# Three rounded products for the attention's output projection, and a subtraction in the vector engine's queue

## What is computed

```
y = num / (den + 1e-6)                       # 16 heads x 64
y = (y - mean(y)) / sqrt(var(y) + 1e-9) * ln_w        # per head
x1 = x + ga * (y.reshape(16 * 64) @ w_proj)  # 1024 -> 256
h  = layernorm(x1) * (1 + cb) + sb
logits = h @ Wr.T                            # 8 experts
```

## Time and profile before

| | us |
|---|---|
| median of 3 runs | 2130.3 (2128.81 to 2131.07) |
| profiled execution, its own time | 2129.61 |
| its span in the profile | 2127.8 |
| PE, DVE, ACT, POOL busy over the span | 1949.6, 1793.2, 1286.0, 830.6 |
| `close_attention`, from the first folding matmul to the last logits copy | 1309.56 to 1525.00 |
| the loop's turns, from tile 8's L1381 to tile 31's | 1358.60 to 1495.45 |

### The profile page before, as it was taken

How to read it: one execution, slowest core, us unless ns; L and a number is a source line. 1 busy time by engine, 2 the same in 40 slices (tenths; PEclk the granted TensorE clock), 3 DMA queues, 4 the chain that set the end, 5 groups by cost and what they waited for, 6 DMA issues and landing times. The chain is left out here.

```text
span 2127.8 us, 37910 instructions
## 1 busy us (share of the span) xinstructions
PE 1949.6 (92%) x13199; PEld 1382.8 (65%) x13199; DVE 1793.2 (84%) x2652; ACT 1286.0 (60%) x2168; POOL 830.6 (39%) x729
## 2 busy tenths in 40 slices
PE   7999779999999999999999995999537999999993
PEld 6767535555555555555555553898526999999993
DVE  5999849999999999999999997777587777787783
ACT  4454357777777787777778772444204565566561
POOL 3777511121111112111111211566345666666563
PEclk9999879999999999999999997999757999999997
DMA  5887892355543345554334502444512443334444
GB/s 181 282 277 268 271 246 55 91 129 124 129 103 99 86 105 130 124 124 91 103 85 120 124 21 86 122 132 131 163 50 55 88 92 79 71 83 90 88 88 109
DMA packets 156104, 260.57 MB, mean 122 GB/s; under 512 B 44568, under 2 KB 120160, under 8 KB 149472
## 3 DMA queue, kind: packets, MB, share of 16 engines
q1 hardware_dynamic: 127792, 214.07, 36.0%
q0 software_dynamic: 15840, 22.29, 6.8%
q10 hardware_dynamic: 12304, 22.02, 3.1%
HBM read 162.40 MB, written 100.14 MB: 123 GB/s over the span
## 5 line engine op out<-in xcount | busy, mean ns | idle before, releaser
L998 ACT ACTIVATE att_sb_a<-att_ps_s,att_sb_fg,att_sb_f 128x1024 f32<-128x1024 f32 x384 | 454.4, 1202 | 230.4 <-PE att_ps_s L1143 219.4
L1036 DVE TENSOR_TENSOR keep_sb_store<-keep_sb_store,att_sb_a 128x1024 f32<-128x1024 f32 (+2 forms) x528 | 535.2, 1028 | 16.6 <-ACT att_sb_a L998 8.3
L954 POOL TENSOR_SCALAR_AFFINE_SELECT att_sb_dec<-att_sb_dec 128x128 f32<-128x128 f32 x256 | 178.7, 699 | 844.9 <-ACT att_sb_dec L988 844.9
L1162 PE MATMUL att_ps_off<-att_sb_a,att_sb_v 128*64 128x512 f32 x1520 | 365.5, 594 | 1.1 <-DVE att_sb_part L1063 1.1
L1795 ACT ACTIVATE ffn_sb_h<-ffn_ps_p,ffn_sb_b_cols 128x256 f32<-128x256 f32 x320 | 152.1, 477 | 168.1 <-PE ffn_ps_p L1986 167.4
L1900 DVE TENSOR_TENSOR ffn_sb_h_lo<-ffn_sb_h,ffn_sb_h_hi 128x256 fp32r<-128x256 f32 x320 | 213.2, 708 | 27.2 <-ACT ffn_sb_h_hi L1788 25.8
L1143 PE MATMUL att_ps_s<-att_sb_q,att_sb_k 64*128 64x512 f32 (+1 forms) x1896 | 229.9, 376 | 5.0 <-DMA att_sb_k<-k_rows 4.9
L1143 PEld LDWEIGHTS att_ps_s<-att_sb_q,att_sb_k 64*128 64x128 f32 x1896 | 159.1, 186 | 115.3 <-issue 63.6
L1143 PEld LDWEIGHTS att_ps_s<-keep_sb_late,att_sb_k 64*128 64x128 f32 x1920 | 160.4, 185 | 110.1 <-issue 56.6
L1143 PE MATMUL att_ps_s<-keep_sb_late,att_sb_k 64*128 64x512 f32 (+3 forms) x1920 | 230.8, 374 | 0.3
L1052 DVE SCALAR_TENSOR_TENSOR att_sb_a<-att_ps_s,att_sb_dec 128x1024 f32<-128x1024 f32 (+3 forms) x256 | 209.0, 817 | 7.7 <-PE att_ps_s L1143 5.3
(11 more groups left out here) (256 smaller groups left out, 3589.3 us busy)
## 6 DMA issues: line engine op xcount, KB each, us to landing
q_rows<-early_sb_halves SPq DMA_DIRECT2D x32, 1024.0 KB, 4.8
att_sb_k<-k_rows SPq DMA_DIRECT2D x60, 512.0 KB, 15.6
ffn_sb_raw<-L_ffn_W ACTq DMA_DIRECT2D x36, 512.0 KB
close_sb_nT<-num_rows SPq DMA_DIRECT2D x34, 512.0 KB, 4.0
k_rows<-early_sb_halves SPq DMA_DIRECT2D x16, 1024.0 KB, 4.9
keep_sb_late<-q_rows SPq DMA_DIRECT2D x32, 512.0 KB, 13.8
num_rows<-att_sb_num SPq DMA_DIRECT2D x64, 256.0 KB, 2.7
att_sb_hb<-half_log SPq DMA_DIRECT2D x15, 1024.0 KB, 22.9
```

What stands on the lines that cost most here:

```text
L954: nc.gpsimd.affine_select(out=tile, in_=tile, compare_op=ALU.is_ge, fill=0.0, base=0, pattern=[[1, P]], channel_multiplier=-1).then_inc(de ...
L998: nc.scalar.activation(x, s_ps[slot(op)][:, :, :], ACT.Square, scale=f[:, p, i - 1, s:s + 1], bias=fg[:, p, i - 1, s:s + 1]).then_inc(sq_d ...
L1036: nc.vector.tensor_tensor(x[:, :, c:TB], x[:, :, c:TB], y[:, :, c:TB], ALU.max).then_inc(max_done, 1)
L1162: last = nc.tensor.matmul(ps[h * HD:(h + 1) * HD, c:TB], v_tile, a[:, a_slot(op), h, c:TB], start=(s == 0), stop=(s == (ST * i if kind == ...
```

## The change

The output projection is computed from three rounded products. `yT` is split into `yT_hi` (ACT's copy, now rounding to float32r) and `yT_lo` (a new subtraction on DVE, `py` minus `yT_hi`, 128x1024). The weights are split into `w_hi` and `w_lo` likewise, by one more DVE instruction for each of the four folded parts. PE does 24 matmuls on float32r in place of eight on float32, of the same shape. PE's next transposes into `py` now wait for the subtraction, as does the projection. In DVE's queue the subtraction stands ahead of the sum of squares. The copy of the logits, which stood there, moves to the end of ACT's turn.

```diff
@@ ACT's turn
-                    nc.scalar.activation(yT[:, p, :, :], py[:, :, :], ACT.Copy).then_inc(yT_done, 1)
+                    nc.scalar.activation(yT_hi[:, p, :, :], py[:, :, :], ACT.Copy).then_inc(yT_hi_done, 1)
...
+                if there[7]:
+                    act.wait_ge(l_mm, ready(n - 7))
+                    apart(act, keep)
+                    nc.scalar.activation(keep.logits[:, n - 7, :], pl[:, :], ACT.Copy).then_inc(l_done, 1)
...
+            act.wait_ge(l_done, ready(NTT - 1))
@@ DVE's fold
-                    nc.vector.tensor_copy(w[:, 2 * g:2 * g + 2, :], pw[:, :, :]).then_inc(folded, 1)
+                    nc.vector.tensor_copy(w_hi[:, at, :], pw[:, :, :]).then_inc(rounded, 1)
+                    dve.wait_ge(rounded, g + 1)
+                    nc.vector.tensor_tensor(w_lo[:, at, :], pw[:, :, :], w_hi[:, at, :].bitcast(F32), ALU.subtract).then_inc(folded, 1)
@@ DVE's turn
-                if there[7]:
-                    dve.wait_ge(l_mm, ready(n - 7))
-                    apart(dve, keep)
-                    nc.vector.tensor_copy(keep.logits[:, n - 7, :], pl[:, :]).then_inc(l_done, 1)
+                if there[2]:
+                    dve.wait_ge(yT_hi_done, ready(n - 2))
+                    dve.wait_ge(a_mm, free(n - 2, 2))
+                    nc.vector.tensor_tensor(yT_lo[:, p, :, :], py[:, :, :], yT_hi[:, p, :, :].bitcast(F32),
+                                            ALU.subtract).then_inc(yT_lo_done, 1)
                 if there[0]:
                     dve.wait_ge(sq_done, ready(n))
@@ PE's turn
-                    pe.wait_ge(yT_done, free(n - 2, 1))
+                    pe.wait_ge(yT_lo_done, free(n - 2, 1))
...
-                    pe.wait_ge(yT_done, ready(n - 3))
+                    pe.wait_ge(yT_lo_done, ready(n - 3))
                     pe.wait_ge(gx_done, free(n - 3, 1))
-                    for j in range(KVH):
-                        last = nc.tensor.matmul(pa[:, :], yT[:, 1 - p, j, :], w[:, j, :], start=(j == 0), stop=(j == KVH - 1))
+                    terms = [(a, b, j) for a, b in ((yT_hi, w_hi), (yT_hi, w_lo), (yT_lo, w_hi)) for j in range(KVH)]
+                    for o, (a, b, j) in enumerate(terms):
+                        last = nc.tensor.matmul(pa[:, :], a[:, 1 - p, j, :], b[:, j, :], start=(o == 0), stop=(o == len(terms) - 1))
```

More of the change, by code:

```diff
@@ L1181, in close_attention @@
         w_raw = m.sbuf("w_raw", [P, KVH, D])
-        w = m.sbuf("w", [P, KVH, D])
+        w_hi = m.sbuf("w_hi", [P, KVH, D], F32R)
+        w_lo = m.sbuf("w_lo", [P, KVH, D], F32R)
         basis_sb = m.sbuf("basis", [P, P])
@@ L1193, in close_attention @@
         y = m.sbuf("y", [P, 2, HEADS, HD])
-        yT = m.sbuf("yT", [P, 2, KVH, P])
+        yT_hi = m.sbuf("yT_hi", [P, 2, KVH, P], F32R)
+        yT_lo = m.sbuf("yT_lo", [P, 2, KVH, P], F32R)
         gx = m.sbuf("gx", [P, 2, D])
@@ L1209, in close_attention @@
         pw = m.psum("pw", [P, 2, D])
-        w_in, scaled, fold_mm, folded, wr_mm, wr_done, eps_done = (
-            m.sem(s) for s in ("w_in", "scaled", "fold_mm", "folded", "wr_mm", "wr", "eps"))
+        w_in, scaled, fold_mm, rounded, folded, wr_mm, wr_done, eps_done = (
+            m.sem(s) for s in ("w_in", "scaled", "fold_mm", "rounded", "folded", "wr_mm", "wr", "eps"))
         n_in = [m.sem(f"n_in{i}") for i in range(2)]
@@ L1214, in close_attention @@
         h_out = [m.sem(f"h_out{i}") for i in range(2)]
-        n_mm, num_done, sq_done, var_done, std_done, r_done, y_done, y_mm, yT_done, a_mm = (
-            m.sem(s) for s in ("n_mm", "num", "sq", "var", "std", "r", "y", "y_mm", "yT", "a_mm"))
+        n_mm, num_done, sq_done, var_done, std_done, r_done, y_done, y_mm, yT_hi_done, yT_lo_done, a_mm = (
+            m.sem(s) for s in ("n_mm", "num", "sq", "var", "std", "r", "y", "y_mm", "yT_hi", "yT_lo", "a_mm"))
         gx_done, x1_done, var2_done, std2_done, xn_done, hs_done, h2_done, h_mm, hT_done, l_mm, l_done, head_chain, norm_chain, mod_chain = (
@@ L1274, in _ @@
         def _(act):
-            for s in (sq_done, std_done, yT_done, std2_done, hT_done):
+            for s in (sq_done, std_done, yT_hi_done, std2_done, hT_done, l_done):
                 act.sem_inc(s, CREDIT)
@@ L1333, in _ @@
         def _(dve):
-            for s in (num_done, var_done, r_done, gx_done, var2_done, xn_done, l_done):
+            for s in (num_done, var_done, r_done, gx_done, var2_done, xn_done, yT_lo_done):
                 dve.sem_inc(s, CREDIT)
@@ L1357, in fold @@
                 for g in parts:
+                    at = slice(2 * g, 2 * g + 2)
                     dve.wait_ge(fold_mm, g + 1)
-                    nc.vector.tensor_copy(w[:, 2 * g:2 * g + 2, :], pw[:, :, :]).then_inc(folded, 1)
+                    nc.vector.tensor_copy(w_hi[:, at, :], pw[:, :, :]).then_inc(rounded, 1)
+                    dve.wait_ge(rounded, g + 1)
+                    nc.vector.tensor_tensor(w_lo[:, at, :], pw[:, :, :], w_hi[:, at, :].bitcast(F32), ALU.subtract).then_inc(folded, 1)
                 if g == KVH // 2 - 1:
```

## The result

The changed kernel takes 2141.43 us (median of 5 runs, 2141.01 to 2143.55), the kernel before 2130.3 us (median of 5, 2128.81 to 2132.72) beside it: a ratio of 1.0054, 95% interval 1.0039 to 1.0068. The change makes the kernel slower by 11.1 us. The profiled execution took 2142.37 us by its own time, with a span of 2140.6 us, 12.8 us more than before.

What follows compares the result with a forecast made beforehand. PE was taken to set the loop's pace at 5.95 us a turn, DVE nearly equal. Loop +18.4, before it +4.4, behind it -0.5 gave +22.3 us, a forecast of 2152.6 us, range 2142 to 2164.

Steps and rivals of the forecast that it cites:

- DVE sets the pace: In the loop: DVE's turn becomes 6.75 us and bounds it; PE's saving of 0.55 us goes into idle time.
- The growth of DVE's turn, 0.80: In the loop: each DVE turn grows from 5.95 to 6.75 us, 0.76 for the subtraction plus 0.04.
- the loop's term: Over the loop's 23 turns, 0.80 us each: +18.4 us.
- The 0.76: In DVE's turn: the sum begins at 1409.92 instead of 1409.16, the subtraction starting where the logits copy did.
- The 0.04 allowed for one more wait: In DVE's turn: a guessed 0.04 us for the one more wait that its queue must evaluate.
- I take these gaps as DVE's own: nothing PE does would close them: DVE's loop idle time, gaps between dependent steps and 0.36 us marked issue, is not slack behind PE.
- DVE's gaps close: Rival, in the loop: issue gaps are covered, the turn grows by 0.4 us, 2143 us in all; chance 0.12.
- The cover of the high part: In the loop: yT_hi is ready 0.5 us before the subtraction wants to begin, so that wait costs nothing.
- the ring that the prediction walked through once, as a check: In the loop: sum, ACT's L1297, logits copy, hT, PE's logits matmuls and transposes of y; yT_hi ready at 2.0 to 2.1.
- Before the loop, +4.4: Ahead of the loop: folded weights +2.3, turns 2 to 4 +0.1, turns 5 and 6 +1.6, turn 7 +0.4 us.
- Behind the loop, -0.5: After the loop: later start and moved copy cost 1.1 us, three shorter projections save 1.65.
- The clock: PE's granted clock stays at 1.00 in the loop; rival: it falls, 2175 to 2245 us, chance 0.05.

Runs made afterwards that it cites:

- e3_dve_alone: Changed kernel with the projection back in eight plain float32 matmuls, the subtraction kept on DVE but its result unused; 2149.35 us, ratio 1.0066.
- e1_apart: Changed kernel with one separate semaphore instruction put in front of the subtraction, as the logits copy had before; 2150.47 us, ratio 1.0059.
- e8_before_unrolled: Kernel before with its 39 turns all written out, no loop; 2131.04 us, ratio 0.9989.
- e13_pe_copy_dve: Changed kernel without y's subtraction, third product taking the high part again, and the logits copy back on DVE; 2131.50 us, ratio 0.9992.
- e9_after_xn_act: Changed kernel with all turns written out and the normalising of x1 moved from DVE to ACT; 2131.72 us, ratio 1.0009.
- e6_logits: Kernel before with only the logits copy moved from DVE to the end of ACT's turn; 2135.32 us, ratio 1.0013.
- e2_pe_alone: Changed kernel without y's subtraction on DVE, the third product taking the high part again; 2135.02 us, ratio 0.9999.
- e4_behind: Changed kernel with the subtraction moved behind the sum of squares on DVE; 2163.47 us, ratio 1.0130.
- e12_before_no_ring: Kernel before, turns written out, x1's normalising on ACT, hT moved behind ACT's squares, logits matmuls to the end of PE's turn; 2160.68 us, ratio 1.0145.

## Why the prediction was right in its sign and wrong in its size

**DVE sets the pace: right.** The turn is the same with PE 0.55 us longer (`e3_dve_alone`), the subtraction takes 1.22 to 1.23 us with a slot of 1.14, and nothing idles before the sum. PE's saving of 0.55 a turn went into PE's wait for `hT`, 1.1 us.

**The growth of DVE's turn, 0.80: wrong, and this is the step that failed.** It measured 0.46, so the loop's term was +10.6 and not +18.4. That is about 8 us of the 9.5 by which the profiled executions differ less than forecast (12.8 and 22.3). Piece by piece, from the timelines of DVE: the sum came later behind L1392 by 1.25 - 0.72 = 0.53 in a turn like that of the earlier trace rows, and by 1.25 - 0.63 = 0.62 in the other; forecast were 0.76. The other turn, before the change:

```profile
1414.36 0.18 DVE L1392 BATCH_NORM_AGGREGATE close_sb_mv<-close_sb_st 128x2 f32<-128x6 f32 x1
1414.62 0.17 DVE L1396 COPY keep_sb_logits<-close_ps_pl 128x8 f32 x1
1414.99 1.20 DVE L1399 TENSOR_REDUCE close_sb_red<-close_sb_sq 128x16 f32<-128x1008 f32 x1 [0.21 <-ACT close_sb_sq L1291]
```

And after it:

```profile
1408.65 0.18 DVE L1402 BATCH_NORM_AGGREGATE close_sb_mv<-close_sb_st 128x2 f32<-128x6 f32 x1
1408.76 1.22 DVE L1406 TENSOR_TENSOR close_sb_yT_lo<-close_ps_py,close_sb_yT_hi 128x1024 fp32r<-128x1024 f32 x1
1409.90 1.20 DVE L1410 TENSOR_REDUCE close_sb_red<-close_sb_sq 128x16 f32<-128x1008 f32 x1
```

The 0.76 came of putting the subtraction where the copy had started, 0.33 us behind L1392. That delay belonged to the copy, to its extra semaphore instruction (`e1_apart`) and its address (`e8_before_unrolled`), and left with it. The 0.04 allowed for one more wait was not needed. And in every second turn 0.26 us of the gap ahead of L1381 closed, of which 0.06 came back at another step. "I take these gaps as DVE's own: nothing PE does would close them" was wrong for that gap: making PE shorter closes it (`e13_pe_copy_dve`), and the ground that the prediction gave for it among its rivals, that `pn` had been ready, holds by 0.1 us only. For the two of about 0.2 in the turns with the loop's branch it was right; they are there after the change as well. The mean: 0.575 + (0.06 - 0.26) / 2 = 0.475, where 0.46 was measured.

The rival called "DVE's gaps close" gave 0.4 a turn and 2143 us, and stood at 0.12. It had the size by luck, and one of the two causes: it closed about 0.4 us in every turn, where 0.26 closed in every second.

**The cover of the high part: right.** 0.20 us of it are left in the loop and the subtraction doesn't wait. In `e9_after_xn_act`, with DVE quicker, it is used up: the ring that the prediction walked through once, as a check, is then the bound.

**Before the loop, +4.4: the sum right by luck, its parts not.** It measured +4.5. The fold cost less, 0.6 + 0.7 + 0 behind the first scaled weights (forecast 2.3); turns 5, 6 and 7 grew by 0.60, 0.35 and 0.29 (forecast 2.0); turns 2 to 4 by nothing (0.1). The rest, 1.9 us, is no price of the change: tile 0's first step came 1.5 us earlier, and the scaling of the weights on DVE then waited for a transfer and for POOL (below). `e6_logits`, which has no part of the fold's change, shows such a start too: its first turn took 14.58 us, and 12.88 in the profile of the kernel before.

**Behind the loop, -0.5: -1.2.** By `e3_dve_alone` the shorter projections save 1.9 us there (forecast 1.65), so the later start and the moved copy cost 0.7 and not the 1.1 allowed.

**The clock: right for the change.** 1.00 in every 10 us of the loop, with PE at 8.0 to 9.2 of 10.

## What to carry to other kernels

An engine at 80% busy whose queue has no long wait is a second bound, but before its gaps are counted as its own, make the first bound shorter and look which of them close: a gap marked issue behind a wait can be the wait. A new step doesn't inherit the start of the step it replaces: a separate semaphore instruction and an address from a register are paid by the instruction that needs them, here 0.07 us for the first and 0.12 to 0.19 for the second, and all that the loop's registers and branch added was 0.5 us of a 6.4 us turn. And when a shorter turn doesn't follow from less work, look for the ring of waits across engines and move a step out of it.

## What was not expected of the hardware

**Whoever starts first holds the other.** The scaling of the weights on DVE, 128x2048 in SBUF, and POOL's `y` run beside each other before the loop. Of the kernel before, DVE and POOL:

```profile
1308.18 1.23 DVE L1356 TENSOR_SCALAR close_sb_w_raw<-close_sb_w_raw,close_sb_lnw 128x2048 f32<-128x2048 f32 x1
```

```profile
1308.35 2.82 POOL L1327 TENSOR_TENSOR close_sb_y<-close_sb_num,close_sb_rinv 128x1024 f32<-128x1024 f32 x1 [11.02 <-DVE close_sb_rinv L1412]
```

And of the kernel after:

```profile
1307.27 2.56 DVE L1363 TENSOR_SCALAR close_sb_w_raw<-close_sb_w_raw,close_sb_lnw 128x2048 f32<-128x2048 f32 x1 [0.51 <-DMA close_sb_wr_raw<-L_ffn_Wr]
```

```profile
1306.85 1.90 POOL L1334 TENSOR_TENSOR close_sb_y<-close_sb_num,close_sb_rinv 128x1024 f32<-128x1024 f32 x1 [11.02 <-DVE close_sb_rinv L1423]
```

DVE began 0.17 us ahead of POOL and took 1.23, and POOL's step took 2.82 instead of 1.90; in the other order POOL took its 1.90 and DVE 2.56, ending 1.08 us behind POOL's end. The Trainium skill ("SBUF — State Buffer", SBUF: two separate sides) says that VectorE, in a mode that uses two ports, and GpSimd share a pair of ports which the one that starts first keeps for its whole instruction, while the other is blocked. Both traces agree with that, to about 0.15 us: behind the end of the first, DVE took 1.08 more us of its 1.23, and POOL 1.76 of its 1.90. That the scaling runs in such a mode no row says; it takes 1.23 us for 2048 elements, as `num` does for 1024. So it works in both directions here. It costs DVE 1.3 us or nothing, by half a microsecond in the start. Nothing of the change decides it: `e2_pe_alone`, whose program is that of the kernel after up to this point, had 1.20 us there, with POOL's `y` at 2.78, and `e6_logits`, whose program is that of the kernel before up to this point, had 2.52 and 1.90.

**The clock dipped once in a loop with more idle time of PE, and it cost nothing.** In `e4_behind`, with the turn at 6.98 us, five stretches of 10 us:

```profile
1390.00:1400.00 10.00, 7.51 (x63) 6.81 (x62) 8.26 (x18) 3.72 (x9) 4.89 (x6) 1.00 0.46 136
1400.00:1410.00 10.00, 8.58 (x64) 7.91 (x63) 8.25 (x19) 4.36 (x8) 6.54 (x7) 0.91 0.31 87
1410.00:1420.00 10.00, 8.76 (x69) 8.31 (x68) 8.27 (x17) 4.63 (x11) 5.50 (x6) 0.92 0.40 116
1420.00:1430.00 10.00, 9.92 (x70) 9.48 (x71) 8.05 (x20) 4.02 (x7) 5.24 (x6) 0.83 0.40 120
1430.00:1440.00 10.00, 8.43 (x71) 7.72 (x69) 7.91 (x17) 4.23 (x8) 6.80 (x7) 1.00 0.35 105
```

The granted clock lies between its two levels for 30 us and is then full again, and PE's busy time grew in them, up to 9.92 of 10. The turns there took 6.84 to 6.85 and 7.12 us, as all others of that loop: PE's idle time took up the loss. The clock's fall that the prediction put at 0.05 exists, then, at a turn 0.57 us longer than the change's. That the idle time brought it is not shown: in `e12_before_no_ring`, with turns of 6.92 us and PE busy 17.4 to 17.9 of 20, the granted clock was 1.00 throughout the loop. The Trainium skill ("TensorE: Matmul & The Clock Gate", A second HAM failure mode: psum-queue depth-cycling) tells of a clock that swings between its levels where PE idles shortly and often between groups of matmuls; this loop shows it in these 30 us alone, and the loop of the changed kernel in none of its rows.
